# Attention stage: block-diagonal direction products as two 64x64 quarters, and the value projection moved two batches ahead, behind the attention weighting

## The chip, the cores and the metric

The kernel runs on one core of one Trainium2 chip. The metric is the device time of one launch in microseconds (us). TensorE (PE) multiplies, VectorE (DVE), ScalarE (ACT) and GpSimd (POOL) do the elementwise work, and each engine runs its own list of instructions in order. They wait for each other through semaphores only.

## The reference, cut to what matters

Two layers (attention and expert network each) are applied to 32 batches of 256 tokens with 128 channels. The change concerns the first layer's attention alone:

```python
q, k, v = heads(xn @ Wq.T), heads(xn @ Wk.T), heads(xn @ Wv.T)      # 8 heads of 16 channels
q, k = _apply_rope(q, cos, sin), _apply_rope(k, cos, sin)
scores = jnp.where(causal, einsum('bhqd,bhkd->bhqk', q, k) * scale, -inf)
out = softmax(scores) @ v
qp = einsum('bhtd,hd->bht', q[..., :3], head_dirs)                  # "geometric" directions
kp = einsum('bhtd,hd->bht', k[..., :3], head_dirs)
geo = jnp.where(causal, qp[..., :, None] * kp[..., None, :], -inf)
out = out + head_scales * (softmax(geo) @ v - out)
x = x + ga * (h + out @ Wo.T)
```

The direction products turn each head's first three channels of q and k into one number per token. All of it is float32.

## The kernel before

The kernel is a row of phases, each with its own block of engine programs: load, attention, route, experts, and then the same for the second layer. `attention_phase` runs from about 97 to 502 us of the span. It loops over the 32 batches `b`; the 8 heads lie as 2 groups of 4, so that one group fills 64 of the 128 rows of TensorE's array. The score, geometric and weighting products are therefore issued as four "quarters" of 64x64 (`tile_position` at 0 or 64 for rows and for columns), while the projections use the whole 128x128 array.

The order of work is written out by hand for each engine. For TensorE, iteration b is:

1. `scores(b, par, 2)`: the last third of the attention scores (L587, L594).
2. `geo(b, par, C, ..)` and `geo(b, par, A, ..)`: geometric scores, units C and A (L611, L617).
3. `front_v(b + 1)`: value projection into `k_wide_ps[:, 0:T]` (L556 by `project`), and `front_geo(b + 1, ..)`: direction products for q (L569) and k (L570) into `q_rows_ps`.
4. `geo(b, par, B_, ..)`: geometric scores, unit B. Its score buffer was last used by unit 2/C, so it waits until ACT has taken the exponentials of unit C (`wait_buffer`).
5. `scores(b + 1, .., 0)` and `scores(b + 1, .., 1)`. The first needs POOL's `spread_queries(b + 1)` (L837, tile `q_diag`), the second a buffer that ACT frees with the exponentials of geometric unit B.
6. `weigh_att(b)`: attention weights times values (L629 on `turned`).
7. `mix(b - 1)`: output product (L647) into `k_wide_ps[:, T:2T]`, `front_qk(b + 2)`: q and k projections (L556).
8. `weigh_geo(b)`: geometric weights times values (L629 on `p_geo`).

Between the engines: after `front_qk(b + 2)`, which stands at the end of iteration b, DVE shuffles and multiplies (L735, L737), POOL rotates (L861, L869), spreads the values (`v_diag`) and then the queries (`q_diag`). After geometric unit C, DVE takes the maxima of score unit 2 (L759, `read_max(b, 2)`), ACT the exponentials of unit 2 (L697), then of geometric units C and A (L688), and after unit B of B. DVE transposes the projected values (L742, `front_v`), ACT scales the mixed output (L710, `gate`), POOL adds it to x (L888).

Of the kernel before, what the change touches and what calls it, by code (L numbers as in the profile page):

```python
# [15 lines left out]
B, T, D = 32, 256, 128  # L16
# [467 lines left out]
PAIRS, HALF = PER // 2, 2 * SLOT  # L484
# [3 lines left out]
def attention_phase(nc, dram, g):  # L488
# [3 lines left out]
    with Scope(nc, "attn") as s:  # L492
        w = s.sb("w", [128, 3, 128])
        wo = s.sb("wo", [128, 128])
        dirs = s.sb("dirs", [128, 2, 128])
# [5 lines left out]
        q, kk = qk[:, :, 0, :], qk[:, :, 1, :]  # L501
# [18 lines left out]
        q_rows_ps, k_wide_ps = (s.ps(name) for name in ("q_rows", "k_wide"))  # L520
        O = s.ps("out", (128, PAIRS, 2 * T))
        k = s.sems("w_in cleared signed ones share_ready qk_made v_made rows_made crossed sines straight qk_ready q_diag v_turned"
                   " v_diag keys_copied key_diag ran_max moving"
                   " att_turned att_weighed geo_weighed recip coef scaled combined out_turned mixed_turned out_made gated"
                   " x_done")
# [5 lines left out]
        both = range(GROUPS)  # L531
# [20 lines left out]
        def _(pe):  # L552
            pe.wait_ge(k.w_in, 64)

            def project(out, n, b):
                return nc.tensor.matmul(out, w[:, n, :], g.xnT[:, tokens(b)], start=True, stop=True)  # L556

            def front_qk(b):
                pe.wait_ge(k.keys_copied, b)
                pe.wait_ge(k.moving, b)  # L560
                project(q_rows_ps[:, 0:T], 0, b)
                project(q_rows_ps[:, T:2 * T], 1, b).then_inc(k.qk_made, 1)

            def front_geo(b, par):
                if b == 0:
                    pe.wait_ge(k.signed, 2)
                pe.wait_ge(k.straight, b + 1)
                pe.wait_ge(k.qk_ready, b + 1)
                nc.tensor.matmul(q_rows_ps[:, 0:T], dirs[:, 0, :], q[:, par, :], start=True, stop=True)  # L569
                nc.tensor.matmul(q_rows_ps[:, T:2 * T], dirs[:, 1, :], kk[:, par, :], start=True, stop=True).then_inc(k.rows_made, 1)  # L570

            def front_v(b):
                pe.wait_ge(k.v_turned, b)
                if b > 2:
                    pe.wait_ge(k.gated, b - 2)
                project(k_wide_ps[:, 0:T], 2, b).then_inc(k.v_made, 1)

            def scores(b, par, u):
                S = buffer(b, u)
                pe.wait_ge(k.q_diag, b + 1)  # L580
                pe.wait_ge(k.qk_ready, b + 1)
                wait_buffer(pe, b, u)
                odd = UNITS[u][1::2]
                for n, c, size in odd:
                    for gr, side, rows, out in quarters:
                        two = S[out, gr, c - size:c + size].rearrange("p (n j) -> p n j", n=2)
                        nc.tensor.matmul(two[:, :, size - 2 * SLOT:size], g.t("spread_bf")[rows, out],  # L587
                                         g.t("mask_pair")[rows, :].rearrange("p (n j) -> p n j", n=2),
                                         start=n == odd[0][0], stop=False, skip_group_check=True,
                                         tile_position=(HALF * gr, HALF * side))  # L590
                for n, c, size in UNITS[u]:
                    for gr, side, rows, out in quarters:
                        seen = SLOT * (n + 1) if n in TRIMMED else size
                        last = nc.tensor.matmul(S[out, gr, c:c + seen], q_diag[rows, par, n, of_side[side]], kk[rows, par, 0:seen],  # L594
                                                start=False, stop=n == UNITS[u][-1][0], skip_group_check=True,
                                                tile_position=(HALF * gr, HALF * side))
                last.then_inc(by_unit[u].made, 1)

            def geo(b, par, u, parts):
                S = buffer(b, u)  # L600
                pe.wait_ge(k.moving, b + 1)
                pe.wait_ge(k.key_diag, b + 1)
                if u != C:
                    wait_buffer(pe, b, u)
                starts = [c for _, c in parts]
                for group in (starts[0:2], starts[2:]):
                    apart = group[1] - group[0] if len(group) == 2 else SLOT
                    for gr, side, rows, out in quarters:
                        if group:
                            own = S[out, gr, group[0]:group[0] + len(group) * apart].rearrange("p (n j) -> p n j", n=len(group))  # L610
                            nc.tensor.matmul(own[:, :, 0:SLOT], g.t("spread_bf")[rows, out],  # L611
                                             g.t("mask_turned")[rows, 0:len(group) * SLOT].rearrange("p (n j) -> p n j", j=SLOT),
                                             start=u != C and group[0] == starts[0], stop=False, skip_group_check=True,
                                             tile_position=(HALF * gr, HALF * side))
                for n, c in parts:
                    for gr, side, rows, out in quarters:
                        last = nc.tensor.matmul(S[out, gr, c:c + WIDE[n]], key_diag[rows, par, n, of_side[side]],  # L617
                                                query_rows[rows, par, SLOT * n:T], start=False, stop=n == parts[-1][0],
                                                skip_group_check=True, tile_position=(HALF * gr, HALF * side))
                last.then_inc(by_unit[u].made, 1)  # L620

            def weigh(kind):
                for n in range(KB):
                    for pair in range(PAIRS):
                        rows = slice(HALF * pair, HALF * pair + HALF)
                        for gr in both:
                            weights = p_geo[rows, gr, GEO_AT[n]:GEO_AT[n] + WIDE[n]] if kind else \
                                turned[rows, gr, n * T + SLOT * n:(n + 1) * T]
                            last = nc.tensor.matmul(O[HALF * gr:HALF * gr + HALF, pair, kind * T + SLOT * n:kind * T + T],  # L629
                                                    v_diag[rows, gr, n], weights,  # L630
                                                    start=n == 0, stop=n == KB - 1, tile_position=(HALF * pair, HALF * gr))
                return last

            def weigh_att(b):
                pe.wait_ge(k.v_diag, GROUPS * (b + 1))
                pe.wait_ge(k.out_turned, b)
                pe.wait_ge(k.att_turned, len(TURNS) * (b + 1))
                weigh(0).then_inc(k.att_weighed, 1)

            def weigh_geo(b):  # L640
                pe.wait_ge(by_unit[B_].exped, b + 1)
                weigh(1).then_inc(k.geo_weighed, 1)

            def mix(b):
                pe.wait_ge(k.v_turned, min(b + 2, B))
                pe.wait_ge(k.mixed_turned, b + 1)
                nc.tensor.matmul(k_wide_ps[:, T:2 * T], wo[:, :], ao[:, :], start=True, stop=True).then_inc(k.out_made, 1)  # L647

# [5 lines left out]
            scores(0, 0, 0)  # L654
            scores(0, 0, 1)
            front_qk(1)
            for b in range(B):
                par = b % 2
                more = b + 1 < B
                scores(b, par, 2)  # L660
                geo(b, par, C, GEO_C)
                geo(b, par, A, GEO_A)
                if more:
                    front_v(b + 1)
                    front_geo(b + 1, 1 - par)
                geo(b, par, B_, GEO_B)
                if more:
                    scores(b + 1, 1 - par, 0)
                    scores(b + 1, 1 - par, 1)
                weigh_att(b)  # L670
                if b > 0:
                    mix(b - 1)
                if b + 2 < B:
                    front_qk(b + 2)
                weigh_geo(b)
            mix(B - 1)

        @block.scalar
# [52 lines left out]
        def _(dve):  # L731
# [6 lines left out]

            def front_v(b):
                dve.wait_ge(k.v_made, b + 1)  # L740
                dve.wait_ge(k.v_diag, GROUPS * b)
                nc.vector.transpose(v_rows[:, :, :, :].rearrange("p n g d -> p (n g d)"), k_wide_ps[:, 0:T]).then_inc(k.v_turned, 1)  # L742

# [64 lines left out]
            for b in range(B):  # L808
                par = b % 2
# [2428 lines left out]
```

## Time and profile before

| | |
|---|---|
| median of 3 runs | 1977.03 us (1974.11 to 1977.23) |
| the profiled execution's own time | 1973.72 us |
| its span, first to last instruction | 1971.9 us |
| PE, DVE, ACT, POOL busy | 82%, 75%, 60%, 55% of the span |
| mean granted TensorE clock | 0.907 of full speed |

The busy shares are means over all phases and say little about the attention alone; the stretch of about 405 us that matters is the one to read. Matmuls are pipelined and their ends are modelled, so for TensorE the distances between starts are read, not the durations. Each float32 matmul shows as two records.

### The profile page before, as it was taken

What the parts mean: (1) busy time and instruction counts of PE and PEld (TensorE: products, weight loads), DVE (VectorE), ACT (ScalarE), POOL (GpSimd) and SP (SyncE); (2) the same over time, 40 slices, a digit from 0 to 9 for tenths busy, and PEclk for the clock granted to TensorE, in tenths of its full rate; (3) what the DMA queues carried; (4) which work ended last, traced back from release to release, by engine and by line L of the source; (5) the groups of instructions that cost most, each with busy time, mean ns of one, the idle gap of its engine ahead of it and who ended that gap; (6) DMA issues with size and microseconds to landing.
All of it is one profiled execution on the core that took longest, in us unless ns stands there. A gap on an engine that the chain in (4) does not pass through costs nothing. (4 is left out here: it accounts for less than half of the span.)

```text
span 1971.9 us, 50860 instructions
## 1 busy us (share of the span) xinstructions
PE 1611.2 (82%) x17727; PEld 1253.2 (64%) x17727; DVE 1473.6 (75%) x4099; ACT 1185.5 (60%) x2763; POOL 1093.7 (55%) x1141
## 2 busy tenths in 40 slices
PE   5599999999689697699847777777789607999995
PEld 5478888887577543344415555555578607999994
DVE  7688888888489743699979999999778624555556
ACT  4566666666279821587737888888466504555552
POOL 3378888887000178233247888888637773444440
PEclk8799999999899789799969999999876658999997
DMA  3000000000511123521000000000321112222217
GB/s 120 19 3 4 3 4 4 3 4 3 209 41 41 33 47 43 149 67 43 12 0 1 1 1 1 1 1 1 128 82 50 52 59 66 66 63 66 66 52 262
DMA packets 84954, 92.34 MB, mean 47 GB/s; under 512 B 11696, under 2 KB 69296, under 8 KB 84000
## 3 DMA queue, kind: packets, MB, share of 16 engines
q1 hardware_dynamic: 67840, 62.66, 10.0%
q0 software_dynamic: 14560, 22.24, 4.2%
q10 hardware_dynamic: 2304, 4.20, 0.6%
q8 instruction: 146, 2.39, 0.5%
q14 instruction: 104, 0.85, 0.1%
HBM read 46.14 MB, written 42.91 MB: 45 GB/s over the span
## 5 line engine op out<-in xcount | busy, mean ns | idle before, releaser
L2284 POOL TENSOR_TENSOR delta_A<-delta_A,delta_sW 128x256 f32<-128x256 f32 x256 | 193.6, 756 | 78.6 <-ACT delta_sW L2131 52.1
L2054 PE MATMUL delta_u<-delta_m,tables_sb 128*128 128x256 f32 x512 | 166.1, 406 | 82.0 <-DVE delta_m L2204 82.0
L697 ACT ACTIVATE attn_p_att<-attn_score,attn_mx 128x32 f32<-128x32 f32 (+7 forms) x512 | 150.2, 409 | 133.7 <-DVE attn_mx L759 133.6
L2911 POOL DMA_INDIRECT choice_rows<-ffn_y,ffn_xg x135 | 129.4, 959 | 167.9 <-DVE ffn_y L3018 164.4
L2131 ACT ACTIVATE delta_sW<-delta_W,tables_sb 128x256 f32<-128x256 f32 x256 | 126.6, 506 | 79.1 <-DVE delta_W L2226 75.2
L2054 PEld LDWEIGHTS delta_u<-delta_m,tables_sb 128*128 128x128 f32 x512 | 87.0, 189 | 132.3 <-DVE delta_m L2204 125.6
L2050 PE MATMUL delta_u<-delta_v_own,tables_sb 128*128 128x256 f32 x512 | 153.6, 382 | 9.6 <-DVE xnT L2191 9.6
L2868 POOL DMA_INDIRECT rows<-mix_rows,mix_slot x128 | 125.4, 979 | 47.0 <-issue 39.4
L1327 POOL DMA_INDIRECT exp_rows<-rows,slot_token x32 | 32.6, 1020 | 190.0 <-issue 190.0
L2226 DVE TENSOR_TENSOR delta_W<-delta_W,delta_u 128x128 f32<-128x128 f32 x512 | 133.6, 282 | 4.5
L2213 DVE TENSOR_TENSOR delta_u<-delta_u,delta_prod 128x256 f32<-128x256 f32 x256 | 109.9, 429 | 17.2 <-PE delta_u L2054 3.3
L2295 POOL TENSOR_TENSOR delta_m<-delta_A,delta_prod 128x768 f32<-128x768 f32 x64 | 122.1, 1908 | 0.0
L3010 DVE TENSOR_TENSOR ffn_hid<-ffn_sg,ffn_val 128x384 f32<-128x384 f32 x135 | 74.9, 554 | 58.1 <-PE ffn_val L2934 58.0
L2122 ACT ACTIVATE delta_v_own<-delta_v_rows,tables_sb 128x256 f32<-128x256 f32 x256 | 113.5, 494 | 0.0
L2934 PE MATMUL ffn_gate<-ffn_xgT,ffn_w_up 128*128 128x128 f32 x810 | 113.3, 276 | 0.0
L2050 PEld LDWEIGHTS delta_u<-delta_v_own,tables_sb 128*128 128x128 f32 x512 | 98.0, 192 | 23.9 <-DVE xnT L2191 10.4
L2934 PE MATMUL ffn_val<-ffn_xgT,ffn_w_up 128*128 128x128 f32 x810 | 113.2, 276 | 0.0
L2945 PE MATMUL ffn_y<-w_down_sb,ffn_hid 128*128 x810 | 112.4, 275 | 0.0
L759 DVE TENSOR_REDUCE attn_mx<-attn_score 128x4 f32<-128x1024 f32 (+3 forms) x128 | 98.4, 807 | 18.5 <-PE attn_score L617 18.0
L2204 DVE TENSOR_TENSOR delta_m<-delta_W,delta_b 128x256 f32<-128x256 f32 x256 | 107.0, 418 | 6.6
L2974 ACT ACTIVATE ffn_w_up<-w_up_sb 128x352 f32 x135 | 67.1, 497 | 67.9 <-PEq L144 43.1
L770 DVE STREAM_TRANSPOSE attn_turned<-attn_p_att 128x1024 f32<-128x1024 f32 (+3 forms) x128 | 101.8, 815 | 0.5 <-ACT attn_p_att L697 0.4
(397 smaller groups left out, 4693.0 us busy)
## 6 DMA issues: line engine op xcount, KB each, us to landing
ffn_xg<-rows SPq DMA_DIRECT2D x135, 66.0 KB, 1.8
acc<-route_zero SPq DMA_DIRECT2D x10, 832.0 KB, 15.5
comb_rows<-choice_rows SPq DMA_DIRECT2D x32, 256.0 KB, 5.2
rows<-route_rows SPq DMA_DIRECT2D x8, 640.0 KB, 3.6
load_rows<-in_x SPq DMA_DIRECT2D x16, 256.0 KB, 3.7
bT<-acc SPq DMA_DIRECT2D x16, 256.0 KB, 3.9
qT<-acc SPq DMA_DIRECT2D x16, 256.0 KB, 4.5
x_kept<-xT SPq DMA_DIRECT2D x16, 256.0 KB, 2.1
```

Of the source, the lines that this page charges most:

```text
L697: last = nc.scalar.activation(p_att[:, gr, PAIR_OFF[n]:PAIR_OFF[n] + SLOT * (n + 1)], S[:, gr, c:c + SLOT * (n + 1)], ACT.Exp, bias=mx[:, ...
L2050: nc.tensor.matmul(corrections(h, pp % 2), g.t("same_head"), moving, start=True, stop=False)
L2054: nc.tensor.matmul(corrections(h, pp % 2), g.t("same_head"), m1[:, h].rearrange("p t d b -> p (t d b)"), start=False, stop=True).then_inc( ...
L2122: ins = nc.scalar.activation(v_own[:, group % AHEAD, d], v_rows[:, group % 2], ACT.Copy, scale=g.t("less_own")[:, d:d + 1])
L2131: nc.scalar.activation(sW[:, step % RING, :], W[:, step % RING].rearrange("p d b -> p (d b)"), ACT.Copy, scale=g.t("step")[:, bass.ds(step ...
L2226: nc.vector.tensor_tensor(W[:, t % RING, :, some(h)], W[:, (t - 1) % RING, :, some(h)], changes(h, pp % 2)[:, n], ALU.subtract).then_inc(b ...
L2284: nc.gpsimd.tensor_tensor(A[:, t % 8], A[:, (t - 1) % 8], sW[:, t % RING], ALU.add).then_inc(k.A, 1)
L2295: nc.gpsimd.tensor_tensor(m3[:, t // QUAD % 2, 0:QUAD - 1], sums, query, ALU.mult).then_inc(k.m3, 1)
L2868: nc.gpsimd.indirect_dma_start(g.rows1, bass.IndirectOffsetOnAxis(slot[:, at:at + 1], 0), rows[:, i % 2, par, j, n, :], None).then_inc(sen ...
L2911: nc.gpsimd.indirect_dma_start(g.choice_rows, bass.IndirectOffsetOnAxis(xg[:, n % RING, D:D + 1].bitcast(U32), 0), y[:, n % RING, :], None ...
L2934: last = nc.tensor.matmul(out[:, 128 * p:128 * p + 128], w_up[:, n % 4, half, 128 * p:128 * p + 128], xgT[:, n % 4, :], start=True, stop=True)
L2945: last = nc.tensor.matmul(y_ps[par][:, 0:D], hid[:, n % 4, 128 * p:128 * p + 128], g.w_down[:, bass.ds(e * P + p, 1), :].rearrange("h o d ...
```

## The change

Three edits in `attention_phase`:

- `front_geo`: the direction matrix `dirs` holds only zeros outside its two diagonal 64x64 blocks (group 0 and group 1). Instead of one full-array matmul for q and one for k, each is issued as two 64x64 quarters at tile positions (0, 0) and (64, 64), 256 columns each.
- `front_v`: the value projection of batch b + 2 is issued in iteration b, between `weigh_att(b)` and `mix(b - 1)`. It was that of batch b + 1, in front of `front_geo(b + 1)`. `front_v(1)` goes to the prologue.
- Waits that follow from it: `front_v` on TensorE waits for the gating one batch less far back (`b - 3`), `mix(b)` waits for one more value transposition and for `gated` of b, and DVE's `front_v` waits for `out_made` and `gated` of two batches ago.

```diff
-                nc.tensor.matmul(q_rows_ps[:, 0:T], dirs[:, 0, :], q[:, par, :], start=True, stop=True)
-                nc.tensor.matmul(q_rows_ps[:, T:2 * T], dirs[:, 1, :], kk[:, par, :], start=True, stop=True).then_inc(k.rows_made, 1)
+                for kind, x in enumerate((q, kk)):
+                    for gr in both:
+                        own = slice(HALF * gr, HALF * gr + HALF)
+                        last = nc.tensor.matmul(q_rows_ps[own, kind * T:(kind + 1) * T], dirs[own, kind, own], x[own, par, :],
+                                                start=True, stop=True, tile_position=(HALF * gr, HALF * gr))
+                last.then_inc(k.rows_made, 1)
 
             def front_v(b):
                 pe.wait_ge(k.v_turned, b)
-                if b > 2:
-                    pe.wait_ge(k.gated, b - 2)
+                if b > 3:
+                    pe.wait_ge(k.gated, b - 3)
                 project(k_wide_ps[:, 0:T], 2, b).then_inc(k.v_made, 1)
...
             def mix(b):
-                pe.wait_ge(k.v_turned, min(b + 2, B))
+                pe.wait_ge(k.v_turned, min(b + 3, B))
+                if b > 0:
+                    pe.wait_ge(k.gated, b)
...
             front_qk(1)
+            front_v(1)
             for b in range(B):
...
                 if more:
-                    front_v(b + 1)
                     front_geo(b + 1, 1 - par)
                 geo(b, par, B_, GEO_B)
...
                 weigh_att(b)
+                if b + 2 < B:
+                    front_v(b + 2)
                 if b > 0:
                     mix(b - 1)
...
             def front_v(b):
                 dve.wait_ge(k.v_made, b + 1)
+                if b > 2:
+                    dve.wait_ge(k.out_made, b - 2)
+                    dve.wait_ge(k.gated, b - 2)
                 dve.wait_ge(k.v_diag, GROUPS * b)
```

## Rows read from the trace of the kernel before

**Rows 1.** Stretches: us, busy of PE, PEld, DVE, ACT, POOL, granted clock, DMA.

```profile
98.00:480.00 382.00, 375.46 (x9316) 304.57 (x9315) 327.82 (x524) 236.23 (x650) 311.75 (x305) 1.00 0.01 4
...
103.00:106.00 3.00, 1.23 (x52) 1.15 (x56) 3.00 (x7) 2.65 (x10) 1.76 (x2) 1.00 0.00 0
```

**Rows 2.** Who waited for whom, 130 to 470 us: total, times, longest.

```profile
ACT attn_p_att L697 <- DVE attn_mx L759: 118.6, 55, 2.4
```

**Rows 3.** One batch on TensorE in order of time: start, duration, instruction, count.

```profile
263.07 2.23 PE L629 MATMUL attn_out<-attn_p_geo,attn_v_diag 64*64 64x256 f32 x64
...
266.01 1.11 PE L617 MATMUL attn_score<-attn_query_rows,attn_key_diag 64*64 64x256 f32 x24
267.05 0.70 PE L556 MATMUL attn_k_wide<-xnT,attn_w 128*128 128x256 f32 x2
267.59 0.59 PE L569 MATMUL attn_q_rows<-attn_qk,attn_dirs 128*128 128x256 f32 x2
268.02 0.59 PE L570 MATMUL attn_q_rows<-attn_qk,attn_dirs 128*128 128x256 f32 x2
268.55 0.24 PE L611 MATMUL attn_score<-tables_bf_sb 64*64 64x64 bf16 x8
...
269.72 0.25 PE L587 MATMUL attn_score<-tables_bf_sb 64*64 64x128 bf16 x4
269.80 0.98 PE L594 MATMUL attn_score<-attn_qk,attn_q_diag 64*64 64x224 f32 x16
270.83 0.31 PE L587 MATMUL attn_score<-tables_bf_sb 64*64 64x128 bf16 x8
...
273.90 0.70 PE L647 MATMUL attn_k_wide<-attn_ao,attn_wo 128*128 128x256 f32 x2
274.43 1.03 PE L556 MATMUL attn_q_rows<-xnT,attn_w 128*128 128x256 f32 x4
275.39 0.66 PE L629 MATMUL attn_out<-attn_p_geo,attn_v_diag 64*64 64x256 f32 x8
```

**Rows 4.** The same batch, first quarters of the attention weighting, two short windows.

```profile
271.77 0.41 PE L629 MATMUL attn_out<-attn_turned,attn_v_diag 64*64 64x256 f32 x4
...
271.99 0.60 PE L629 MATMUL attn_out<-attn_turned,attn_v_diag 64*64 64x256 f32 x8
```

**Rows 5.** The same batch on the other engines.

```profile
262.41 0.50 ACT L710 ACTIVATE attn_gated<-attn_k_wide,mod 128x256 f32<-128x256 f32 x1
...
266.20 0.69 DVE L759 TENSOR_REDUCE attn_mx<-attn_score 128x4 f32<-128x512 f32 x1 [0.55 <-PE attn_score L617]
...
271.51 0.41 DVE L742 STREAM_TRANSPOSE attn_v_rows<-attn_k_wide 128x256 f32<-128x256 f32 x1
...
266.99 1.09 ACT L697 ACTIVATE attn_p_att<-attn_score,attn_mx 128x96 f32<-128x96 f32 x4 [2.12 <-DVE attn_mx L759]
...
267.95 0.45 ACT L688 ACTIVATE attn_p_geo<-attn_score 128x320 f32<-128x320 f32 x1
...
269.72 0.97 ACT L688 ACTIVATE attn_p_geo<-attn_score 128x960 f32<-128x960 f32 x1 [0.40 <-PE attn_score L617]
...
267.74 1.92 POOL L837 TENSOR_TENSOR attn_q_diag<-attn_qk,tables_sb 128x1024 f32<-128x1024 f32 x1
```

**Rows 6.** The last batch (b = 31), which has no front work: PE, then ACT.

```profile
484.07 2.23 PE L629 MATMUL attn_out<-attn_p_geo,attn_v_diag 64*64 64x256 f32 x64
...
489.55 0.24 PE L611 MATMUL attn_score<-tables_bf_sb 64*64 64x64 bf16 x8 [1.35 <-ACT attn_p_geo L688]
...
488.95 0.45 ACT L688 ACTIVATE attn_p_geo<-attn_score 128x320 f32<-128x320 f32 x1
```

**Rows 7.** A batch in which ACT came late: PE (two short windows), then ACT.

```profile
225.70 0.45 PE L629 MATMUL attn_out<-attn_p_geo,attn_v_diag 64*64 64x256 f32 x4
...
231.45 0.24 PE L611 MATMUL attn_score<-tables_bf_sb 64*64 64x64 bf16 x8 [0.21 <-ACT attn_p_geo L688]
...
230.85 1.37 ACT L688 ACTIVATE attn_p_geo<-attn_score 128x320 f32<-128x320 f32 x2
```

## The prediction

> **What bounds the kernel now.** I read the busy time by stretches first. In the attention loop TensorE is busy for 375 of 382 us at the full granted clock [rows 1], far ahead of the next engine, POOL. That invites the reading "TensorE is the bound, so work taken off it or a mode change saved is time gained". A busy share of 98% does not prove it, because the modelled ends of the matmuls run into the next start and hide short stalls. So I read the table of waits next, for a wait of another engine that hides a chain: ACT waits 118.6 us in 340 for the maxima of DVE [rows 2]. Then one batch in order of time on every engine, which decides.
>
> One batch lasts 275.39 - 263.07 = 12.32 us, from one geometric weighting to the next [rows 3]. Follow what releases each step:
>
> - The geometric scores of unit B start at 268.55 [rows 3]. They need the buffer that ACT frees with the exponentials of unit C. That instruction starts at 267.95 and takes 0.45, so it ends at 268.40 [rows 5]; the start comes 0.15 later.
> - TensorE itself reaches this point at about the same time. Its last direction product starts at 268.02 and lasts two records of 0.215, to 268.45; with the change of array mode that follows (0.10, below) that is again 268.55 [rows 3]. The two releases coincide, so this batch alone cannot tell which one holds.
> - Two other batches can. The last one has no value projection and no direction products before unit B, and TensorE sits idle for 1.35 us with ACT named as releaser. Yet unit B starts at 489.55 - 484.07 = 5.48 us after the geometric weighting [rows 6], and in the full batch at 268.55 - 263.07 = 5.48 us too [rows 3]. Exponentials C start 4.88 us after it in both (488.95 and 267.95) [rows 5, 6]. In the other, ACT came 0.27 late: exponentials C start 230.85 - 225.70 = 5.15 us after the geometric weighting, and unit B starts 231.45 - 225.70 = 5.75 after it, 0.27 late as well [rows 7].
>
> So unit B is released by a chain that bypasses the front work: geometric weighting, score unit 2, unit C on TensorE, maxima on DVE (266.20), exponentials on ACT (266.99, then C) [rows 5]. After unit B two more releases come from outside. Score unit 0 starts at 269.72, when POOL ends q_diag at 267.74 + 1.92 = 269.66 [rows 3, 5]. Score unit 1 starts at 270.83, when ACT ends exponentials B at 269.72 + 0.97 = 270.69 [rows 3, 5]; TensorE was done with unit 0 about 0.2 us earlier (by the spacing of its records, near 270.62). From 270.83 to the next unit C there is no outside release: score unit 1, attention weighting, output product, q and k projections, geometric weighting follow each other. Every microsecond put there lengthens the batch.
>
> **The change part by part.** *The value projection leaves the stretch before unit B.* A full-array product of 256 columns takes 268.02 - 267.59 = 0.43 us between two others of its kind [rows 3]. There it was covered by the ACT chain, as the last batch shows, so taking it away gives 0. TensorE waits instead.
>
> *The value projection enters between the attention weighting and the output product.* Its new neighbour is a full-array product, so it costs the same 0.43, on the path. The lower bound is 0.43; the upper bound is 0.53, the distance of the output product to the next (274.43 - 273.90) [rows 3], which is what a product beside a change of mode costs. The change of mode is there already and is only passed on, so I take 0.43. It runs for b = 0 to 29: 30 x 0.43 = 12.9 us. The same distance is what the mode change from quarters to full array costs, 0.10, plus what the gap before the first record costs: unit A has 2 x (256 + 224 + 32) columns, 0.86 us at 0.215 per 256, from 266.01 to 266.87 or slightly more, and the projection starts at 267.05, so about 0.12. From full array to quarters: four records of q and k cost 0.86, the distance is 275.39 - 274.43 = 0.96, so 0.10 [rows 3]. One round trip is 0.32.
>
> *The direction products in quarters.* Four quarters of 256 columns start at 271.77 and their second records at 271.99 [rows 4]: quarters that share neither place run side by side at the same 0.22 per record as the full array. Two diagonal quarters of q then take 0.43 and of k 0.43, 0.86 in all, as now. Nothing in the trace shows two quarters only. If they did not overlap it would be 4 x 0.43 = 1.72; below 0.86 they would gain nothing, since they end early anyway. They start after unit A near 266.93 (q and k were rotated for this batch before that) and end at 267.79, or at 268.65 in the worst case, against the release that lets unit B start at 268.55. I take 0.86, as four quarters overlap; cost 0 while the ACT chain covers them, and 0.1 us per batch, 31 x 0.1 = 3.1 us, at the other end. DVE reads the direction rows only after it has ended other work, so their being early helps nobody.
>
> *The mode changes.* One round trip of two goes: 0.32 us per batch. It lies in the covered stretch, and its worth is 0 for the same reason.
> The Trainium skill says in "TensorEngine Tiling (Array Packing)", section Key Properties, that changing the tiling mode drains TensorE. The 0.32 agrees that this costs something. By that rule alone the change would be a gain of 0.32 us per batch; it speaks for the second rival below, and the sum here does without it.
>
> *The waits.* TensorE's projection waits for gated of two batches before; queued behind it are the output product and the q and k projections, and DVE and POOL wait for those. ACT's gating of a batch comes at 262.41 + 0.50 [rows 5], some 11 us earlier than the projection that needs it. The output product waits for the value transposition of 271.51 + 0.41 = 271.92 and would start near 274.3, 2.4 us later [rows 5]. DVE's transposition waits for the output product and gating of the batch before, done by 262.91, at 271.51; the maxima behind it are not held up. All cost 0.
>
> *Prologue.* The extra projection falls into TensorE's empty stretch before the first loop pass, where it is busy for 1.23 of 3 us [rows 1]: 0.
>
> Sum: 30 x 0.43 = +12.9 us. What is late next does not change: all three releases hang on the q and k projections and the geometric weighting, which now come 0.43 later in each batch. The profiled execution has 1973.7, of which 1.8 lies outside its span of 1971.9, so it would become 1986.6, its span 1984.8. The median would become 1989.9. The four executions of before lie in two pairs near 1974 and 1977; I put my number on their mean of 1975.5: 1988.4.
>
> **The rivals.**
>
> *Quarters side by side only in fours.* The worst case above: +12.9 + 3.1 = +16.0, 1991.5. For it: no row shows two alone. Against: in fours they start within hundredths of each other.
>
> *TensorE is the bound, faster.* The two releases of unit B coincide in full batches, and one may argue that ACT's chain follows TensorE. Then the batch loses projection and round trip in front (-0.43 - 0.32) and gains 0.43: -0.32 x 30 = -9.6, 1965.9. It decides if both the exponentials C and q_diag can come earlier than they do. Against it: the last batch and the late batch, and POOL's 269.66, which depends on the q and k projections alone.
>
> *Half of that.* If only the release of unit B moves with TensorE, q_diag still holds unit 0 at 269.72, and unit 1 starts at 270.62 instead of 270.83. The batch changes by -0.21 + 0.43 = +0.22: +6.6, 1982.1. Only the coincidence speaks for it.
>
> *The change does nothing measurable.* The 0.43 would have to be taken up by slack in the stretch after 270.83. DVE waits there about 1 us for the q and k projections, but that is DVE waiting for TensorE, so it is slack of the wrong engine. Time 1975.5.
>
> *The clock falls.* TensorE would wait about 0.76 us more per batch, and a fall to 1.2 GHz for a tenth of the loop would add up to some 38 us: about 2027. Against it: in the loop's start TensorE is busy for 1.23 of 3 us and the granted clock stays at 1.00 [rows 1], the 2.4 GHz level.
>
> **How the numbers follow.** Chances: forecast 0.72, quarters not overlapping 0.08, half 0.07, clock 0.05, faster 0.04, no change 0.04. Forecast and the quarters' rival hold 0.80. The forecast's own spread is the two pairs of runs (1.6 to either side) and later phases whose clock pattern may shift a little, 2 us: 1984.5. At the top 1991.5 plus 1.5: 1993.0. What can be told from no change is about 0.2%, 4 us. Slower by more than that: forecast, quarters, half and clock, 0.92; same 0.04; faster 0.04.
>
> **What would show it.** In the trace of after a batch lasts 12.75 us. TensorE idles for about 0.75 us before unit B (L611) with ACT's p_geo as releaser, unit B still starts 5.48 us after the geometric weighting, score unit 1 still 7.76 after it. From the last attention weighting to the next geometric weighting there are two more full-array records, 0.43 in all. Direction products: eight records of 64x64 in 0.86 us. I am wrong if unit B starts earlier than 5.4 us after the geometric weighting, if exponentials C come earlier than 4.88, or if the eight records take over 1.6 us.

## The result

The changed kernel takes 1987.59 us (median of 4 runs, 1986.35 to 1990.43) against 1975.57 us of the kernel before (4 runs). The ratio is 1.0065, 95% interval 1.0048 to 1.0081: slower by 12.0 us, a small change (0.65%) but clear of the spread. The forecast was 1988.4 us, +12.9.

The page of the changed kernel: the span, and each engine's busy time with its instructions.

```profile
span 1985.9 us, 51144 instructions
PE 1606.2 (81%) x17855; PEld 1246.0 (63%) x17855; DVE 1473.0 (74%) x4099; ACT 1188.7 (60%) x2763; POOL 1094.5 (55%) x1141
```

TensorE has less busy time than before (1606 against 1611 us) in a longer span: TensorE does the same work and waits more. One batch on TensorE, in order of time; it answers to [rows 3].

```profile
269.32 2.23 PE L633 MATMUL attn_out<-attn_p_geo,attn_v_diag 64*64 64x256 f32 x64
...
272.26 1.11 PE L621 MATMUL attn_score<-attn_query_rows,attn_key_diag 64*64 64x256 f32 x24
273.19 1.07 PE L572 MATMUL attn_q_rows<-attn_qk,attn_dirs 64*64 64x256 f32 x8
274.80 0.24 PE L615 MATMUL attn_score<-tables_bf_sb 64*64 64x64 bf16 x8 [0.54 <-ACT attn_p_geo L696]
274.87 1.03 PE L621 MATMUL attn_score<-attn_query_rows,attn_key_diag 64*64 64x192 f32 x24
275.98 0.25 PE L591 MATMUL attn_score<-tables_bf_sb 64*64 64x128 bf16 x4
...
277.08 0.31 PE L591 MATMUL attn_score<-tables_bf_sb 64*64 64x128 bf16 x8
...
280.14 0.70 PE L556 MATMUL attn_k_wide<-xnT,attn_w 128*128 128x256 f32 x2
280.68 0.59 PE L653 MATMUL attn_k_wide<-attn_ao,attn_wo 128*128 128x256 f32 x2
281.11 1.03 PE L556 MATMUL attn_q_rows<-xnT,attn_w 128*128 128x256 f32 x4
282.06 0.45 PE L633 MATMUL attn_out<-attn_p_geo,attn_v_diag 64*64 64x256 f32 x4
```

The batch lasts 282.06 - 269.32 = 12.74 us, 0.42 more than in [rows 3]. Unit B (L615 at 274.80) starts 5.48 us after the geometric weighting, as in [rows 3] and [rows 6], although the work in front of it has shrunk by a value projection and a round trip of modes. TensorE now waits there with ACT named: for 0.54 us by the modelled ends of its products, for 274.80 - 273.19 - 0.86 = 0.75 us by their starts (0.86 is the work of the direction quarters). Score unit 1 (277.08) comes at 7.76, also as before. The new time lies in the full-array block between the two weightings, which has eight records where it had six, the value projection at 280.14 being new: it lasts 282.06 - 280.14 = 1.92 us, and lasted 275.39 - 273.90 = 1.49 [rows 3].

The releases of that batch on ACT and POOL (they answer to [rows 5]).

```profile
274.20 0.46 ACT L696 ACTIVATE attn_p_geo<-attn_score 128x320 f32<-128x320 f32 x1
...
273.99 1.93 POOL L848 TENSOR_TENSOR attn_q_diag<-attn_qk,tables_sb 128x1024 f32<-128x1024 f32 x1
```

Exponentials C start 274.20 - 269.32 = 4.88 us after the weighting (before 4.88) and end 0.14 before unit B starts. POOL ends q_diag at 275.92, score unit 0 starts at 275.98. Who waited for whom between 130 and 480 us shows the new wait as 28 waits of TensorE for ACT in front of L615, 15.3 us in total. Over the same stretch of the kernel before, TensorE's products waited for ACT in front of unit B once, for 0.2 us, and its weight loads (PEld) sat idle there for 9.9 us.

```profile
PEld attn_score L615 <- issue: 27.2, 28, 1.2
...
PE attn_score L615 <- ACT attn_p_geo L696: 15.3, 28, 0.8
```

From the first to the last attention weighting the trace of after has 392.58 us, that of before 379.64: 12.94 more. The profiled spans differ by 14.0; 0.8 of the rest arises before the attention begins (its first product starts at 91.9 instead of 91.1). That start lies anywhere from 89.1 to 91.9 in the traces here, whatever the edit. For that reason the experiments are read by the batch first: "batch" is the median distance from one attention weighting to the next in a kernel's trace. The kernel before ran beside each group of experiments, with medians of 1972.5 to 1975.5 us; the ratios are to those runs.

### The profile page after: what moved, and what is told of

Read it like the earlier page. It is cut to its first block and busy times, and to the rows that moved or that the text cites. A ratio compares the mean times of both kernels' runs of the same rounds, so it can differ in the third digit from the quotient of the medians.

```text
span 1985.9 us, 51144 instructions
## 1 busy us (share of the span) xinstructions
PE 1606.2 (81%) x17855; PEld 1246.0 (63%) x17855; DVE 1473.0 (74%) x4099; ACT 1188.7 (60%) x2763; POOL 1094.5 (55%) x1141
## 5 line engine op out<-in xcount | busy, mean ns | idle before, releaser
L2945 PEld LDWEIGHTS ffn_gate<-ffn_xgT,ffn_w_up 128*128 128x128 f32 x810 | 102.1, 193 | 0.0
```

What stands on the lines that cost most here:

```text
L2945: last = nc.tensor.matmul(out[:, 128 * p:128 * p + 128], w_up[:, n % 4, half, 128 * p:128 * p + 128], xgT[:, n % 4, :], start=True, stop=True)
```

## The experiments

| kernel | batch, us | median, us | ratio to before, 95% |
|---|---|---|---|
| before | 12.32 | 1975.57 | 1 |
| after | 12.74 | 1987.59 | 1.0065 [1.0048, 1.0081] |
| quarters only | 12.34 | 1974.26 | 1.0006 [0.9990, 1.0021] |
| move only | 12.73 | 1984.94 | 1.0056 [1.0037, 1.0074] |
| before, no projection in the loop | 12.30 | 1971.37 | 0.9989 [0.9976, 1.0003] |
| after, no projection in the loop | 12.30 | 1971.68 | 0.9992 [0.9978, 1.0006] |
| after, q products twice | 12.74 | 1988.99 | 1.0080 [1.0058, 1.0101] |
| after, weighting behind unit C | 12.50 | 1980.27 | 1.0029 [1.0019, 1.0039] |
| before, weighting behind unit C | 12.28 | 1973.05 | 0.9992 [0.9983, 1.0001] |
| after, weighting behind unit C, queries first | 12.26 | 1974.18 | 1.0001 [0.9989, 1.0013] |
| the same, and maxima of unit 0 first | 12.07 | 1968.86 | 0.9979 [0.9964, 0.9994] |
| after, reordered | 11.50 | 1950.10 | 0.9872 [0.9857, 0.9887] |
| before, reordered | 11.77 | 1958.26 | 0.9921 [0.9908, 0.9935] |

### Each part alone

**Quarters only.** The kernel before with this edit alone:

```diff
-                nc.tensor.matmul(q_rows_ps[:, 0:T], dirs[:, 0, :], q[:, par, :], start=True, stop=True)
-                nc.tensor.matmul(q_rows_ps[:, T:2 * T], dirs[:, 1, :], kk[:, par, :], start=True, stop=True).then_inc(k.rows_made, 1)
+                for kind, x in enumerate((q, kk)):
+                    for gr in both:
+                        own = slice(HALF * gr, HALF * gr + HALF)
+                        last = nc.tensor.matmul(q_rows_ps[own, kind * T:(kind + 1) * T], dirs[own, kind, own], x[own, par, :],
+                                                start=True, stop=True, tile_position=(HALF * gr, HALF * gr))
+                last.then_inc(k.rows_made, 1)
```

> Kernel before with the quarters alone; the value projection stays in front of the direction products. Theory (unit B is released by ACT's exponentials of unit C, not by TensorE): the batch stays at 12.32 us, unit B still starts 5.48 us after the geometric weighting, time within 0.2% of before. Rival (TensorE's front work is the bound): the number of mode changes is the same as before, so about the same time too, unless the quarters are slower than two full products, then up to +0.86 us per batch, +27 us.

TensorE in one batch of it:

```profile
264.42 2.23 PE L633 MATMUL attn_out<-attn_p_geo,attn_v_diag 64*64 64x256 f32 x64
...
269.02 1.08 PE L572 MATMUL attn_q_rows<-attn_qk,attn_dirs 64*64 64x256 f32 x8
269.89 0.26 PE L615 MATMUL attn_score<-tables_bf_sb 64*64 64x64 bf16 x8
...
276.76 2.23 PE L633 MATMUL attn_out<-attn_p_geo,attn_v_diag 64*64 64x256 f32 x64
```

The eight records take 269.89 - 269.02 = 0.87 us, the same as the two full products. Unit B keeps its place (269.89 - 264.42 = 5.47), the batch is 0.03 longer than before (12.344 against 12.316), and the time is that of before. That quarters overlap only in fours is ruled out.

**Move only.** The changed kernel with the two full-array direction products back in place of the quarters.

> Changed kernel with full-array direction products: only the value projection is moved. Theory: 12.74 us per batch as in the changed kernel, +12 to +13 us on before, since the mode changes left in front of unit B are covered. Rival (TensorE's front work is the bound, the quarters save one round trip of modes): 0.32 us per batch slower than the changed kernel, about +10 us on it.

```profile
268.32 2.23 PE L629 MATMUL attn_out<-attn_p_geo,attn_v_diag 64*64 64x256 f32 x64
...
273.79 0.24 PE L611 MATMUL attn_score<-tables_bf_sb 64*64 64x64 bf16 x8 [0.36 <-ACT attn_p_geo L692]
```

12.73 us: the whole loss comes from the move. The round trip of modes that is left in front of unit B (still at 273.79 - 268.32 = 5.47) costs nothing; the wait behind it is merely shorter, 0.36 instead of 0.54.

### The same work at two places

**The projection taken out at its old place.** It is left out of the kernel before for all batches but the first, so every batch weights the values of the first one.

```diff
                 if more:
-                    front_v(b + 1)
                     front_geo(b + 1, 1 - par)
...
-                dve.wait_ge(k.v_made, b + 1)
+                dve.wait_ge(k.v_made, 1)
```

> Kernel before without the value projection in the loop (left out for all batches but the first, so every batch uses the values of the first). Theory: 12.32 us per batch, unit B still 5.48 us after the geometric weighting, with TensorE idle for 0.4 us more in front of it; time within 0.2% of before. Rival (TensorE is the bound): -0.43 us per batch, -13 us. Rival in between (only unit B follows TensorE): -0.21 us per batch, -6.5 us.

```profile
261.83 2.23 PE L629 MATMUL attn_out<-attn_p_geo,attn_v_diag 64*64 64x256 f32 x64
...
267.31 0.24 PE L611 MATMUL attn_score<-tables_bf_sb 64*64 64x64 bf16 x8 [0.36 <-ACT attn_p_geo L687]
...
274.14 2.23 PE L629 MATMUL attn_out<-attn_p_geo,attn_v_diag 64*64 64x256 f32 x64
```

Without 0.43 us of TensorE work per batch the batch is 274.14 - 261.83 = 12.31, and unit B still starts at 5.48. This separates the two releases that coincide in [rows 3]: with TensorE ready earlier, ACT's release alone holds unit B at the same place.

**And taken out at its new place.** The changed kernel without `front_v(b + 2)` in the loop and `front_v(1)` ahead of it, with the same wait on DVE.

> Changed kernel without the value projection in the loop (left out for all batches but the first). Theory: the projection costs its full 0.43 us where it now stands, so the batch falls from 12.74 to 12.31 us and the time from +12 to about that of before. Rival (the loss comes from the new waits or from the quarters): the batch stays above 12.5 us.

```profile
262.07 2.23 PE L633 MATMUL attn_out<-attn_p_geo,attn_v_diag 64*64 64x256 f32 x64
...
267.54 0.24 PE L615 MATMUL attn_score<-tables_bf_sb 64*64 64x64 bf16 x8 [0.53 <-ACT attn_p_geo L693]
...
274.38 2.23 PE L633 MATMUL attn_out<-attn_p_geo,attn_v_diag 64*64 64x256 f32 x64
```

12.31 again, with unit B at 267.54 - 262.07 = 5.47. By the medians the same two records are worth 12.316 - 12.304 = 0.01 at the old place and 12.740 - 12.304 = 0.44 at the new one. The added waits and the quarters, which are all still there, cost nothing.

**Work added in front of unit B.** The changed kernel with the quarter products of q issued twice.

```diff
-                for kind, x in enumerate((q, kk)):
+                for kind, x in ((0, q), (0, q), (1, kk)):
```

> The changed kernel with the two quarter products of q issued twice, +0.43 us of TensorE work in front of unit B. Theory: it goes into TensorE's wait of 0.7 us there and costs nothing, 12.74 us per batch, same time as the changed kernel. Rival (TensorE's work counts wherever it stands): 13.17 us per batch, +13 us on the changed kernel.

```profile
271.15 2.23 PE L633 MATMUL attn_out<-attn_p_geo,attn_v_diag 64*64 64x256 f32 x64
...
275.02 1.51 PE L572 MATMUL attn_q_rows<-attn_qk,attn_dirs 64*64 64x256 f32 x12
276.63 0.24 PE L615 MATMUL attn_score<-tables_bf_sb 64*64 64x64 bf16 x8
...
283.89 2.22 PE L633 MATMUL attn_out<-attn_p_geo,attn_v_diag 64*64 64x256 f32 x64
```

Twelve records instead of eight, unit B at 5.48, batch 12.74: the stretch takes 0.43 us of work for nothing.

### Moving the releases

If the chain through ACT holds unit B, letting it begin earlier must help the changed kernel and not the one before. Two kernels carry this edit:

```diff
                 geo(b, par, C, GEO_C)
+                if b > 0:
+                    weigh_geo(b - 1)
                 geo(b, par, A, GEO_A)
...
                     front_qk(b + 2)
-                weigh_geo(b)
+            weigh_geo(B - 1)
             mix(B - 1)
```

> Changed kernel, and TensorE's geometric weighting of batch b-1 moved behind score unit 2 and geometric unit C of batch b, so that the chain maxima - exponentials C starts earlier. Theory: unit B is released 0.3 to 0.55 us earlier; score unit 0 is then held by POOL's q_diag at its old place, unit 1 starts right behind it, 0.2 us earlier; batch 12.74 - 0.2 = 12.54 us, about -6 us on the changed kernel. Rival (the release of unit B does not matter): 12.74 us.

The changed kernel with it; score unit 2 now opens the batch.

```profile
265.42 0.25 PE L591 MATMUL attn_score<-tables_bf_sb 64*64 64x128 bf16 x4
...
270.22 0.24 PE L615 MATMUL attn_score<-tables_bf_sb 64*64 64x64 bf16 x8
...
272.06 0.25 PE L591 MATMUL attn_score<-tables_bf_sb 64*64 64x128 bf16 x4 [0.74 <-POOL attn_q_diag L850]
...
272.95 0.28 PE L591 MATMUL attn_score<-tables_bf_sb 64*64 64x128 bf16 x8
...
277.92 0.25 PE L591 MATMUL attn_score<-tables_bf_sb 64*64 64x128 bf16 x4
```

> The same edit on the kernel before. There TensorE itself reaches unit B only at the time of the old release, so the earlier release brings nothing: 12.32 us per batch, within 0.2% of before. Rival: -0.2 us per batch, as in the changed kernel.

The kernel before with it: the same three starts.

```profile
272.99 0.25 PE L587 MATMUL attn_score<-tables_bf_sb 64*64 64x128 bf16 x4
...
278.42 0.24 PE L611 MATMUL attn_score<-tables_bf_sb 64*64 64x64 bf16 x8
279.63 0.25 PE L587 MATMUL attn_score<-tables_bf_sb 64*64 64x128 bf16 x4
```

Both are read from the first product behind the q and k projections, which was the geometric weighting and is now score unit 2. In the changed kernel unit B moves from 5.48 to 270.22 - 265.42 = 4.80 us, and the wait turns up in front of score unit 0 with POOL's q_diag as releaser, at 272.06 - 265.42 = 6.64, where [rows 3] has 6.65. Unit 1 follows unit 0 at once. The batch falls by 0.24 (0.20 expected). In the kernel before unit B starts at 278.42 - 272.99 = 5.43, only 0.05 earlier than without the edit, because there TensorE arrives only then, and the batch falls by 0.03 (12.316 to 12.283). So the coincidence of the two releases is real to within 0.05 us: in the kernel before, ACT's release alone puts unit B at 5.48, TensorE's own work alone at 5.43.

**Taking q_diag out as well.** On the changed kernel with the weighting behind unit C, POOL spreads queries before values.

```diff
             for b in range(B):
...
-                spread_values(b)
                 if more:
                     spread_queries(b + 1, 1 - par)
+                spread_values(b)
```

> The changed kernel with geometric weighting behind unit C, and on top POOL spreading the queries before the values, so that q_diag ends 1.18 us earlier. Theory: the release by q_diag is gone, score unit 0 follows unit B, unit 1 waits for ACT's exponentials of unit B, 0.46 us earlier than without this edit: 12.50 - 0.46 = 12.04 us per batch, about -14 us on that kernel. Rival (POOL's order does not matter, TensorE or DVE holds): 12.50 us.

A miss: 12.26 instead of 12.04. Three TensorE rows and one of DVE from its trace.

```profile
269.51 0.31 PE L591 MATMUL attn_score<-tables_bf_sb 64*64 64x128 bf16 x8 [0.24 <-ACT attn_p_geo L698]
...
273.54 1.03 PE L556 MATMUL attn_q_rows<-xnT,attn_w 128*128 128x256 f32 x4
274.78 0.25 PE L591 MATMUL attn_score<-tables_bf_sb 64*64 64x128 bf16 x4 [0.21 <-ACT attn_p_att L707]
...
271.47 0.45 DVE L800 STREAM_TRANSPOSE attn_ao<-attn_aoT 128x256 f32<-128x256 f32 x1 [0.89 <-POOL attn_aoT L868]
```

No wait for q_diag is left among TensorE's products, but with everything earlier, DVE reaches the transposition of the mixed rows before POOL has them and stands still for 0.89 us, the maxima of unit 0 queued behind. ACT's exponentials of unit 0 are late by that, and TensorE waits at 274.78. I had named what frees score unit 1 but not what is queued behind the next wait on DVE. The test of that reading puts the maxima of unit 0 in front of the transposition:

```diff
+                if more:
+                    read_max(b + 1, 0)
                 if b > 0:
                     turn_mixed(b - 1)
                 if more:
-                    read_max(b + 1, 0)
                     read_max(b + 1, 1)
```

> The previous reordered kernel (geometric weighting behind unit C, queries first), which came to 12.26 us per batch instead of 12.04. Its trace shows DVE waiting 0.89 us for POOL's mixed rows in front of the maxima of score unit 0, and TensorE then waiting for ACT's exponentials of unit 0. Here the maxima of unit 0 are put in front of that transposition. Theory (that queue is the cause): the wait in front of score unit 2, about 0.28 us, goes, 11.95 to 12.0 us per batch. Rival (the cause is ACT's late exponentials of unit B): stays at 12.26 us.

```profile
268.14 0.31 PE L591 MATMUL attn_score<-tables_bf_sb 64*64 64x128 bf16 x8 [0.30 <-ACT attn_p_geo L698]
...
272.61 1.03 PE L556 MATMUL attn_q_rows<-xnT,attn_w 128*128 128x256 f32 x4
273.56 0.25 PE L591 MATMUL attn_score<-tables_bf_sb 64*64 64x128 bf16 x4
```

The wait in front of score unit 2 is gone (273.56 carries none): from the q and k projections to score unit 2 it takes 273.56 - 272.61 = 0.95 us instead of 274.78 - 273.54 = 1.24. The batch falls by 0.19 to 12.07, about two thirds of the fall expected (to 11.95 or 12.0). Part of the gain goes into the wait for the exponentials of unit B in front of score unit 1, which this edit does not touch and which grows from 0.24 to 0.30. So the queue on DVE is shown as the cause of the wait in front of score unit 2.

What that is worth in time is not shown. In the profiled execution about half of the batches are longer than 12.07, up to 13.20 us; in six of them the attention weighting alone takes 2.56 to 3.26 us instead of 2.12, with no releaser named, and why is open. From the first attention weighting to the last geometric weighting it has 382.2 us, no less than the 381.5 of the kernel without this last edit. The medians of the times lie 5.3 us apart (1974.18 and 1968.86), but the 7.5 us between the two profiled spans arise almost wholly behind the attention (1482.1 and 1475.0 us), where the two kernels are the same.

**All releases out of the way.** On top of the last edits, unit B is issued before the direction products, DVE takes the maxima of unit 2 before its first transposition, and does its remaining transpositions before the scan (`front_moving`). The same reordering is applied to the changed kernel and to the one before, which keeps value projection and full-array direction products together in front of score unit 0.

```diff
                 geo(b, par, A, GEO_A)
-                if more:
-                    front_geo(b + 1, 1 - par)
                 geo(b, par, B_, GEO_B)
                 if more:
+                    front_geo(b + 1, 1 - par)
                     scores(b + 1, 1 - par, 0)
...
+                read_max(b, 2)
                 turn_att(b, *TURNS[0])
-                read_max(b, 2)
...
                 turn_att(b, *TURNS[1])
-                if more:
-                    front_moving(b + 1, 1 - par)
                 turn_att(b, *TURNS[2])
                 turn_att(b, *TURNS[3])
                 if more:
+                    front_moving(b + 1, 1 - par)
                     front_v(b + 1)
```

> Changed kernel with all three releases moved out of TensorE's way: geometric weighting of b-1 behind unit C, maxima of unit 2 before the first transposition on DVE, unit B before the direction products, queries spread before values on POOL, DVE's remaining transpositions before the scan, maxima of unit 0 before the mixed transposition. Theory: score unit 1 starts right behind unit 0, TensorE hardly idles, batch near 11.95 us (12.74 less 0.76 idle before unit B and the small gaps), -11 us on before. Rival (DVE, at 10.7 us per batch, or its order becomes the bound): 12.2 us or more.

The reordered changed kernel on TensorE:

```profile
265.80 0.25 PE L591 MATMUL attn_score<-tables_bf_sb 64*64 64x128 bf16 x4
...
269.70 1.01 PE L621 MATMUL attn_score<-attn_query_rows,attn_key_diag 64*64 64x192 f32 x24
270.55 1.03 PE L572 MATMUL attn_q_rows<-attn_qk,attn_dirs 64*64 64x256 f32 x8
271.42 0.25 PE L591 MATMUL attn_score<-tables_bf_sb 64*64 64x128 bf16 x4
...
272.32 0.28 PE L591 MATMUL attn_score<-tables_bf_sb 64*64 64x128 bf16 x8
...
277.28 0.25 PE L591 MATMUL attn_score<-tables_bf_sb 64*64 64x128 bf16 x4
```

> The same reordering on the kernel before: value projection and full-array direction products stand between unit B and score unit 0. Theory: TensorE is now the bound, so the change's saved round trip of modes is worth its 0.32 us per batch: about 12.27 us here against 11.95 in the reordered changed kernel, that is the sign of the change turns over, about 10 us in its favour. Rival (the round trip costs nothing anywhere): both the same.

The reordered kernel before:

```profile
267.45 0.25 PE L587 MATMUL attn_score<-tables_bf_sb 64*64 64x128 bf16 x4
...
271.36 1.01 PE L617 MATMUL attn_score<-attn_query_rows,attn_key_diag 64*64 64x192 f32 x24
272.30 0.70 PE L556 MATMUL attn_k_wide<-xnT,attn_w 128*128 128x256 f32 x2
...
273.27 0.59 PE L570 MATMUL attn_q_rows<-attn_qk,attn_dirs 128*128 128x256 f32 x2
273.80 0.25 PE L587 MATMUL attn_score<-tables_bf_sb 64*64 64x128 bf16 x4
...
279.22 0.25 PE L587 MATMUL attn_score<-tables_bf_sb 64*64 64x128 bf16 x4
```

TensorE's products carry no wait in either batch; in the stretch from 130 to 460 us they are busy for 329.4 and 330.0 of 330 us. The busy share alone would not prove it; the starts agree: score unit 0 comes 0.87 us after the direction quarters begin, which is their work, and unit 1 comes 0.90 after unit 0, where the changed kernel has 1.10. Batches: 11.50 and 11.77. The expected values were too high by 0.45 and 0.50. For the changed kernel I had taken off its wait before unit B, 0.75, and forgotten most of the two smaller ones. By the starts they are 0.26 in front of score unit 0 (unit B to unit 0 takes 275.98 - 274.87 = 1.11 us in the changed kernel, and unit B 270.55 - 269.70 = 0.85 here) and 0.20 in front of unit 1 (277.08 - 275.98 = 1.10 against 272.32 - 271.42 = 0.90). With them the sum is 12.74 - 0.75 - 0.26 - 0.20 = 11.53. The difference that was the point of the pair came as forecast in sign and nearly in size: 0.27 us per batch in favour of the change (0.32 expected), 1950.1 against 1958.3 us. From the first products of unit B to score unit 0 the changed kernel needs 271.42 - 269.70 = 1.72 us, the other 273.80 - 271.36 = 2.44; of the 0.72 it pays 0.43 back in the block after the attention weighting. What is left is the round trip: in the reordered kernel before, 272.30 - 271.36 - 0.85 = 0.09 us in front of the first full-array product and 273.80 - 273.27 - 0.43 = 0.10 on the way back are such costs, and the rest lies between the first two full-array products.

The reordered changed kernel is the fastest of all: 1950.1 us, ratio to before 0.9872 (0.9857 to 0.9887). Most of that comes from the reordering, which on the kernel before gives 0.9921.

## Why the prediction was right

**What bounds the batch.** Right, and shown. Unit B starts 5.48 us after the geometric weighting with more work ahead of it (q products twice), with less (no projection) and with the change. The chain through ACT was read from the last and the late batch of the profile before [rows 6, 7]; the experiments confirm that reading and rule out both rivals in which unit B follows TensorE. In the kernel before, TensorE itself is ready at most 0.05 us before ACT's release, so the chain holds there by a narrow margin; that more work in front of unit B would have counted there is argued and was not run.

**The projection leaves the front: 0.** Right: 12.30 us without it altogether, against 12.32.

**The projection enters the block: 30 x 0.43.** Right in mechanism; the size measured is 12.74 - 12.32 = 0.42 per batch. By the experiments that is 0.44 at the new place less 0.01 at the old one. Over the loop 12.94 us against the 12.9 of the sum, single longer batches included.

**Quarters: 0.86 us, cost 0.** Right; eight records in 0.87 us, where they stand without a wait behind them (quarters only, and the reordered changed kernel).

**Mode changes: one round trip of 0.32, worth 0 here.** Worth 0 is shown by "move only", which keeps the round trip and takes no more time than the change. Its price was somewhat too high: where it counts, the pair of reordered kernels differs by 0.27 per batch. That pair differs in the form of the direction products too, but these take 0.87 us in quarters and 0.86 as full products.
The Trainium skill says in "TensorEngine Tiling (Array Packing)", section Key Properties, that a change of tiling mode drains TensorE. The pair agrees that a change costs time, 0.27 us for a round trip; that it is a drain, no row shows. A gain of the whole change by that rule did not come (slower by 12.0 us), because the round trip stood in covered time.

**The waits: 0.** Right: the changed kernel without the projection keeps them all and runs in 12.30.

**Clock.** The granted clock stayed at 1.00 in the loop, the 2.4 GHz level, with TensorE busy for 321.8 of 340 us (130 to 470 us). The fall of the clock, one of the rivals, did not occur.

**The number.** 1988.4 forecast, 1987.6 measured. The growth of the loop, 12.94 us, is what the forecast was about. That the medians agree to 0.8 us is in part luck: the runs of the changed kernel spread over 4.1 us, and the base of 1975.5 was a mean chosen from four executions, where the kernel before later had medians from 1972.5 to 1975.6.

## What to carry to other kernels

An engine that is 98% busy may still not be what holds an iteration: look for the waits that coincide with its work, and for iterations that lack that work (the last one, a late one) to tell the two apart. Work in front of such a release is free as long as TensorE is done before it (0.43 us more fitted into the changed kernel's 0.75), and taking it away gains nothing; the same work behind it counts in full. Whether moving work pays depends on where the releases stand: here the same change costs 12 us with them closed and gains 8 us with them open. And a release that is opened uncovers the next one: here q_diag, and then what was queued behind a waiting instruction of DVE.

## What the runs showed of the hardware

- Two 64x64 quarters on the diagonal, float32, 256 columns each, run side by side as four do: q and k, four products, take 0.87 us (quarters only, and the reordered changed kernel), as much as two full-array products (0.86). Here, using half the array's quarters costs no time and saves none.
- Going from quarters to the full array and back cost 0.27 us of TensorE time at the granted clock of 1.00 where nothing covers it (11.77 against 11.50 us per batch), and nothing where it stood in front of a release that came later (12.73 against 12.74).
